# One fused layer: seven small projections moved into TensorE's first wait, scores a turn later, the trace inputs on VectorE alone

## The chip, the cores and the metric

The kernel runs on one core of a Trainium2 chip. The metric is device time in microseconds (us) for one launch; the lower the better. Three runs of the kernel before gave 239.74, 240.85 and 242.25 us, median 240.85.

## The reference, cut to what matters

Eight batches (B = 8) of 128 tokens with 128 channels. The layer has four parts:

```python
# 1 cross attention, 16 heads of 8, masked, plus one "self" score per query
s = softmax([q @ k_prev.T * SCALE masked, (q * k_self).sum(-1) * SCALE])
a = (s[..., :-1] @ v_prev + s[..., -1:] * v_self) @ Wo + bo
# 2 windowed attention (16 tokens back, sigmoid weights), then a layer norm
x1 = x + layernorm(window_attention(a)) * gamma + beta
# 3 conditioning: gate from x1 and its decayed context, modulation from a small network,
#   eight decayed traces over the tokens, each of gate * x1 * modulation_d * blend_d
gated = sigmoid(concat(x1, ctx) @ Wg + bg) * x1          # per token and channel
mod   = sigmoid(gelu(x1 @ Wn1 + bn1) @ Wn2 + bn2) + 0.5    # eight numbers per token
trace = sum_d ema_d(gated * mod[d] * blend[d])   # d = 0..7
z = layernorm((gelu(x1 @ Wsoma) * sigmoid(trace @ Wtemp)) @ Wout)
# 4 a mixture of 8 experts, one per token: out = x1 + gate * ffn_e(z)
```

The change touches parts 1 and 3.

## The kernel before, in words

All engines run hand-written instruction streams that meet at semaphores. There is one list of PSUM jobs, `order`: each small job on TensorE (PE) has a bank and a place in that bank's queue, and waits until the job before it on the bank has been read.

**Front.** Both halves of the batches (four each) are transposed, projected to q and k, split into three bf16 parts by ScalarE (ACT) and VectorE (DVE), and stacked by DMAs from SyncE's queue (SP, L398), 12 for each half. PE may start the first scores only when the stack of half 0 has landed.

**First attention.** A loop over turns `t` does one group of four heads of one batch in each step: `scores_max` (unit t, PE L694), whose row maximum DVE takes (`row_max`, L1436); `scores` (unit t - 8, L717), whose exponential ACT takes (`weights_of`, L1157); `values` (unit t - 10, L731). After the four maxima of a batch DVE computes the negated maximum (`shift`, L1442 to L1444), PE turns it (`turn_shift`, L704, last but the projections in turn 4b + 4), ACT copies it and issues a DMA (L1167) that writes it into the stack; the first `scores` of that batch waits for this DMA (`shift_in`). The list `PREPARE` puts seven jobs of the front into turns 0 to 9: the self scores of both halves (`self_0`, `self_1`, L658), the value projections of both inputs and halves (`vp`, `vs`, L666) and the self k projection of half 1 (`ks_1`, L628). At t = 30 the first half goes over to the window attention (`HANDOFF`), whose stack SP builds anew. The turns go on into the window attention (L829, L832, L843) at `WINDOW_AT`.

**Conditioning.** Of half 0 the transposes, context, gate and hidden jobs lie in the last turns of the window attention. After them PE runs `soma(0)`, `modulation(0)` (L863), `traces(0)` (L907: 8 products of 128x128 in f32, 16 records, per batch), then for half 1 `transpose_x1`, `context`, `hidden`, `soma`, then `traces(1)`, `modulation(1)`, `input_gate(1)` and `traces(2)` to `traces(7)`, with output jobs between them. The inputs of the traces, `Gb`, have four buffers for eight batches. DVE writes six of the eight slices of each (`blended`, L1565, one scalar_tensor_tensor per slice), GpSimd (POOL) the other two in one pair of tensor_tensor (L578, L579; `PD = 2`). `traces(b)` waits for both. On DVE the order is `mod_sums(0)`, `modulate(0)`, `blended(0)`, `add_norm(1)` (the second half of the layer norm: L1511, L1514, L1515), `blended(1)` to `blended(7)`, with the sums of gate and modulation of half 1 after `blended(3)`.

**Rest.** Layer norm, router, a scatter of the rows by expert through memory, and 15 expert tiles.

Of the kernel before, what the change touches and what calls it, by code (L numbers as in the profile page):

```python
# [14 lines left out]
def fused_layer(nc, A, out):  # L15
# [27 lines left out]
    with ctx:  # L43
# [42 lines left out]
        prodT = sb("prodT", [128, HT])  # L86
# [122 lines left out]
        PD = 2  # L209

        GROUPS = (range(0, HALF), range(HALF, NB - 1), range(NB - 1, NB))

        LAG_SCORES, LAG_VALUES = 8, 10
        LAG_PVTR, LAG_OUT = 12, 15
# [3 lines left out]
        PREPARE = {0: "self_0", 1: "vp_0", 2: "vs_0", 3: "ks_1", 7: "self_1", 8: "vp_1", 9: "vs_1"}  # L218
# [11 lines left out]
        def handoff(t, step):  # L230
# [5 lines left out]
                 ("kT_1", 3), ("ks_0", 7)]  # L236
        alternating = []
        for t in range(TURNS):
            if t in PREPARE:
                alternating += [PREPARE[t]]  # L240
# [16 lines left out]
        alternating += ["mod_0", "x1T_1", "ctxT_1", "h1_1", "mod_1", "gate_1",  # L257
# [78 lines left out]
        blend_vector, blend_pool, blend_used, traces_read = sem("blend_vector"), sem("blend_pool"), sem("blend_used"), sem("traces_read")  # L336
# [125 lines left out]
        def _(pool):  # L462
# [106 lines left out]
            job_wait_read(pool, "bl_0")  # L569
            job_wait_read(pool, "bl_1")  # L570
            for b in range(NB):
                k = b % NG
                pool.wait_ge(gated_ready, half_of(b) + 1)
                pool.wait_ge(mod_ready, half_of(b) + 1)
                if b >= NG:
                    pool.wait_ge(blend_used, b - NG + 1)
                ds = slice(ND - PD, ND)
                link(pool.tensor_tensor(Gb[:, k, ds, :], bc_mid(wgate[:, b, :], PD), blend[:, ds, :], ALU.mult))  # L578
                pool.tensor_tensor(Gb[:, k, ds, :], Gb[:, k, ds, :], bc_last(mod[:, b, ds], D), ALU.mult)\  # L579
                    .then_inc(blend_pool, 1)  # L580

# [37 lines left out]
        def _(pe):  # L619
# [32 lines left out]
            def sum_self(half):  # L652
                name = f"self_{half}"
                job_wait_read(pe, f"ks_{half}")
                pe.wait_ge(heads_ready, 1)
                job_wait_free(pe, name)
                for i in range(HALF):
                    m = pe.matmul(bank_of(name)[:, i * H:(i + 1) * H], prodT[:, i * T:(i + 1) * T], heads[:],  # L658
                                  start=True, stop=True)
                job_full(m, name)  # L660
# [45 lines left out]
            def scores(b, g):  # L706
                u = b * G + g
                pe.wait_ge(shift_in[b % 2], 16 * (b // 2 + 1))
                if u == 0:
                    job_wait_read(pe, "qT_1")  # L710
                    job_wait_read(pe, "kT_1")
# [8 lines left out]
            def values(b, g):  # L720
                u = b * G + g
                pe.wait_ge(scores_read, u + 1)
                if u == 0:
                    job_wait_read(pe, "trS2_1")
                    job_wait_read(pe, "trX_1")
# [68 lines left out]
            def prepare(name):  # L794
                what, half = name.split("_")
                half = int(half)
                if what == "ks":
                    project_self_k(half)
                if what == "self":
                    sum_self(half)  # L800
                if what == "vp":
                    job_wait_read(pe, f"trX_{half}")
                    pe.wait_ge(ld_wv, 16)
                    four_batches(name, half, xT, wqkv[:, 2, :])
                if what == "vs":
                    job_wait_read(pe, f"trS2_{half}")
                    four_batches(name, half, s2T, wqkv[:, 2, :])
# [8 lines left out]
            project_self_k(0)  # L816

# [80 lines left out]
            def traces(b):  # L898

                pe.wait_ge(blend_vector, b + 1)  # L900
                pe.wait_ge(blend_pool, b + 1)
# [20 lines left out]
            for t in range(TURNS):  # L922
                if t < UNITS:
                    scores_max(t // G, t % G)
                if t in PREPARE:
                    prepare(PREPARE[t])
# [14 lines left out]
                if t >= NEGM_AT and t % G == 0 and t <= UNITS:  # L941
                    turn_shift(t // G - 1)
# [116 lines left out]
        def _(act):  # L1059
# [159 lines left out]

            act.wait_ge(tau_abs, 1)  # L1220
# [4 lines left out]
            for t in range(TURNS):  # L1225
                for half, name in ((int(n[-1]), n[:2]) for n in (PREPARE.get(t - 1),) if n):
                    if name == "vp":
                        evac_prev_v(half)
                    if name == "vs":
                        evac_self_v(half)  # L1230
# [61 lines left out]
            gelu("soma_1", somaT, 128, BSOMA, 1)  # L1292
            mod_sigmoid(1)
            gate_sigmoid(1)
# [57 lines left out]
        def _(dve):  # L1352
# [50 lines left out]
            def self_product(half):  # L1403

                name = f"ks_{half}"
                job_wait_full(dve, name)
                if half:
                    job_wait_read(dve, "self_0")
                job_read(dve.scalar_tensor_tensor(prodT[:], bank_of(name)[:, 0:HT], cols[:, BK:BK + 1], whole(0, half),
                                                  ALU.add, ALU.mult), name)  # L1410
# [16 lines left out]
            self_product(0)  # L1427

# [129 lines left out]
            def blended(b):  # L1558
# [5 lines left out]
                for d in range(ND - PD):  # L1564
# [11 lines left out]
            for t in range(TURNS + 1):  # L1576
# [8 lines left out]
                if t == G:  # L1585
                    self_product(1)
                if t == 2 * G:
# [148 lines left out]
```

## Time and profile before

| | us |
|---|---|
| runs shown, lowest, median, highest | 239.74, 240.85, 242.25 |
| profiled execution, its own time | 243.61 |
| its span, first to last instruction | 241.9 |
| busy: PE, DVE, ACT, POOL | 179.5, 117.8, 114.9, 74.1 |
| mean granted TensorE clock | 0.852 |

The profiled execution is 2.76 us longer than the median of the three runs shown. Busy shares are averages over the whole span; the rows read for the prediction are from single stretches, in us from the start of the span.

### The profile page before, as it was taken

Reading aid. Unit: us, or ns where it says so; the run is one execution under the profiler, and the core shown is the slowest. Engines: PE = TensorE matmul, PEld = TensorE weight load, DVE = VectorE, ACT = ScalarE, POOL = GpSimd, SP = SyncE. Lnnn points to the kernel's source line nnn. Section 1 sums busy time; section 2 is a strip of 40 time slices with the busy share of each in tenths; the row PEclk is TensorE's granted clock in tenths of the full one; section 3 lists DMA queues with packets and bytes.
Section 4 is the critical chain, followed back from the end, with each engine's and each line's share of the span. In section 5 each row is a group of like instructions: output and inputs, shape, how many; then the busy total and the mean of one; then the engine's idle time right before and its main releaser. Section 6 shows DMA issues by size and latency. Waiting matters only on the chain.

```text
span 241.9 us, 4780 instructions
## 1 busy us (share of the span) xinstructions
PE 179.5 (74%) x1677; PEld 136.0 (56%) x1677; DVE 117.8 (49%) x337; ACT 114.9 (48%) x268; POOL 74.1 (31%) x109
## 2 busy tenths in 40 slices
PE   3771986989979779996999649949951005999990
PEld 2321955767645545653567347948751004999990
DVE  6455391566873631431153598396367101455530
ACT  3664142578757677761555506301374001455550
POOL 8996002000700040000200370070256740155553
PEclk9976595899999799997999959977995555899997
DMA  4455354560000440250000893000000229100000
GB/s 125 112 135 169 101 173 113 155 182 3 7 3 1 144 128 3 84 166 16 3 3 0 297 313 87 0 0 3 0 3 0 87 87 299 42 25 24 24 9 0
DMA packets 21085, 18.91 MB, mean 78 GB/s; under 512 B 4029, under 2 KB 18608, under 8 KB 21062
## 3 DMA queue, kind: packets, MB, share of 16 engines
q1 hardware_dynamic: 19606, 16.86, 23.3%
q0 software_dynamic: 896, 1.59, 1.9%
q8 instruction: 14, 0.23, 0.4%
q10 hardware_dynamic: 560, 0.16, 0.3%
q14 instruction: 9, 0.07, 0.1%
HBM read 8.54 MB, written 4.03 MB: 52 GB/s over the span
## 4 chain that ended last, share of the span: by engine, by line
PE 51%; DMA 15%; SPq 10%; DVE 9%; ACT 4%; issue 4%; POOL 4%; ACTq 0%; DVEq 0%; POOLq 0%
SPq L398 9%; PE ps L1052 6%; PE ps L1039 6%; PE ps L907 5%; DMA t_Ks<-t_parts 5%; PE ps L863 5%; DMA t_Qs<-t_negmT 5%; DVE t_Qs L1565 4%; PE ps L628 4%; PE ps L843 3%; POOL z_dram L606 3%; PE ps L829 3%; PE ps L694 2%; PE ps L731 2%; PE ps L666 2%
## 5 line engine op out<-in xcount | busy, mean ns | idle before, releaser
L1347 ACT ACTIVATE t_v_pad<-ps,t_b_tile 128x128 f32<-128x128 f32 x60 | 17.1, 368 | 33.2 <-PE ps L1039 33.2
L1436 DVE TENSOR_REDUCE t_mx<-ps 128x4 f32<-128x512 f32 x32 | 21.8, 688 | 20.8 <-PE ps L694 20.7
L1189 ACT ACTIVATE t_P<-ps 128x512 f32<-128x512 f32 x32 | 19.1, 603 | 15.3 <-PE ps L832 14.9
L907 PE MATMUL ps<-t_ema,t_Qs 128*128 128x128 f32 x128 | 19.2, 317 | 8.4 <-DVE t_Qs L1565 8.4
L907 PEld LDWEIGHTS ps<-t_ema,t_Qs 128*128 128x128 f32 x128 | 18.6, 230 | 10.5 <-DVE t_Qs L1565 9.4
L1157 ACT ACTIVATE t_P<-ps 128x512 f32<-128x512 f32 x32 | 18.9, 605 | 10.1 <-PE ps L717 5.3
L611 POOL DMA_INDIRECT out_dram<-t_v_pad,t_Qs x15 | 15.1, 1008 | 25.9 <-DVE t_v_pad L1710 25.3
L1565 DVE SCALAR_TENSOR_TENSOR t_Qs<-t_v_pad,t_mod,t_blend 128x128 f32<-128x128 f32 x48 | 19.4, 478 | 0.2
L563 POOL TENSOR_SCALAR t_rstd<-t_mv 128x4 f32<-128x4 f32 (+2 forms) x5 | 1.4, 276 | 55.9 <-DVE t_mv L1505 55.9
L694 PE MATMUL ps<-t_Ks,t_Qs 96*128 96x128 bf16 x128 | 13.9, 237 | 6.0 <-DMA t_Ks<-t_parts 5.3
L1039 PE MATMUL ps<-t_zsT,t_late 128*128 128x128 f32 x120 | 17.7, 296 | 0.2 <-DVE t_zsT L1706 0.2
L1031 PE MATMUL ps<-t_ident,t_Qs 128*128 128x128 f32 x15 | 4.4, 308 | 17.5 <-DMA t_Qs<-z_dram 17.5
L1052 PE MATMUL ps<-t_Ks,t_v_pad 128*128 x120 | 17.0, 286 | 0.0
L1039 PEld LDWEIGHTS ps<-t_zsT,t_late 128*128 128x128 f32 x120 | 16.2, 210 | 0.6 <-DVE t_zsT L1706 0.6
L829 PE MATMUL ps<-t_bandb,t_identb 128*128 128x512 bf16 x32 | 12.8, 400 | 4.2 <-DMA t_Ks<-t_parts 4.2
L694 PEld LDWEIGHTS ps<-t_Ks,t_Qs 96*128 96x128 bf16 x128 | 9.7, 109 | 10.5 <-issue 8.6
L1052 PEld LDWEIGHTS ps<-t_Ks,t_v_pad 128*128 128x128 f32 x120 | 15.0, 196 | 0.3
L717 PE MATMUL ps<-t_Qs,t_Ks 96*128 96x128 bf16 x128 | 13.3, 230 | 2.4 <-DMA t_Qs<-t_negmT 1.4
L843 PE MATMUL ps<-t_P,t_v_pad 128*32 128x128 f32 x256 | 13.7, 290 | 0.0
L731 PE MATMUL ps<-t_P,t_v_pad 128*32 128x128 f32 x256 | 13.6, 289 | 0.0
L832 PEld LDWEIGHTS ps<-t_Qs,t_Ks 96*128 96x128 bf16 x128 | 10.3, 100 | 5.0 <-issue 1.2
L832 PE MATMUL ps<-t_Qs,t_Ks 96*128 96x128 bf16 x128 | 12.9, 225 | 0.0
(266 smaller groups left out, 376.3 us busy)
## 6 DMA issues: line engine op xcount, KB each, us to landing
t_Qs<-t_parts SPq DMA_DIRECT2D x24, 128.0 KB
t_Ks<-t_parts SPq DMA_DIRECT2D x24, 128.0 KB
t_Ks<-in_L_ffn_W_dram SPq DMA_DIRECT2D x1, 2048.0 KB, 9.6
z_dram<-t_empty_row SPq DMA_DIRECT2D x1, 1935.0 KB, 8.3
t_Qs<-z_dram SPq DMA_DIRECT2D x1, 1032.0 KB, 7.9
t_Qs<-z_dram SPq DMA_DIRECT2D x1, 645.0 KB, 5.5
t_rows<-in_fside_BxSxS_dram SPq DMA_DIRECT2D x2, 256.0 KB, 3.1
t_x_tok<-in_x_dram SPq DMA_DIRECT2D x2, 256.0 KB, 3.6
```

Of the source, the lines that this page charges most:

```text
L398: sp.dma_start(stack[2 * slot:KROWS:SPAN, half], parts[:, half, which, part, :])\
L694: m = pe.matmul(MAX_BANKS[u % 2][:, j * T:(j + 1) * T], stacked(Qs, b, h), stacked(Ks, b, h), start=True, stop=True)
L829: pe.matmul(bank[:, :], identb[:], bc_mid(bandb[:], 4), start=True, stop=False)
L832: m = pe.matmul(bank[:, j * T:(j + 1) * T], stacked(Ks, b, h), stacked(Qs, b, h), start=False, stop=(j == 3))
L843: m = pe.matmul(VALUE_BANKS[b % 2][32 * j:32 * j + 32, 0:T], v_pad[:, b, quad_head(g, j), :], P[:, (UNITS + u) % 3, j * T:(j + 1) * T], st ...
L907: m = pe.matmul(ps[group][:, i * T:(i + 1) * T], Gb[:, b % NG, d, :], ema[:, 1 + d, :], start=(d == 0), stop=(d == ND - 1))
L1039: m = pe.matmul(ps[n % 2][:, c * 128:(c + 1) * 128], W1_tile[:, n % 2, c * 128:(c + 1) * 128], zsT[:, n % 2, :], start=True, stop=True)
L1052: m = pe.matmul(o, hsT[:, n % 2, c * 128:(c + 1) * 128], W2[:, bass.ds(e, 1), c, :].rearrange("p a f -> p (a f)"), start=False, stop=(c == ...
L1157: act.activation(P[:, u % 3, :], SCORE_BANKS[u % 2][:, :], ACT.Exp, scale=SCALE).then_inc(scores_read, 1)
L1189: act.activation(P[:, (UNITS + u) % 3, :], ps[u % 4][:, :], ACT.Sigmoid, scale=SCALE).then_inc(window_scores_read, 1)
L1436: dve.tensor_reduce(mx[:, b, 4 * g:4 * g + 4], MAX_BANKS[u % 2][:, :].rearrange("p (j t) -> p j t", j=4), AX.X, ALU.max).then_inc(max_scor ...
L1565: m = dve.scalar_tensor_tensor(Gb[:, b % NG, d, :], wgate[:, b, :], mod[:, b, d:d + 1], blend[:, d, :], ALU.mult, ALU.mult)
```

## The change

- `PREPARE` is gone. PE does its seven jobs right after `project_self_k(0)`, ahead of turn 0, in the order vp_0, ks_1, vs_0, vp_1, vs_1, self_0, self_1. ACT copies the four value projections ahead of its turns, DVE forms both self products ahead of its turns and reads the second self scores at t = 2 in place of t = 8. `prodT` has a buffer for each half. Banks 2 to 7 serve the seven jobs.
- All lags of the first attention grow by one turn: scores 9, values 11, output steps 13 and 16 turns behind the maxima.
- `turn_shift` is ahead of `values` in its turn, where it was behind `values` and the window work.
- DVE writes all eight slices of `Gb`; POOL's loop, its semaphore and PE's wait on it are gone.
- DVE does `add_norm(1)` ahead of `blended(0)`; after `blended(3)` the gate's sum stands ahead of the modulation's; ACT's two sigmoids of half 1 change places too.
- PE does `modulation(0)` ahead of `soma(0)`, then all jobs of half 1 (transposes, context, hidden, gate, modulation, soma), and then the eight traces in a row with the output jobs between them as they were.

```diff
-        LAG_SCORES, LAG_VALUES = 8, 10
-        LAG_PVTR, LAG_OUT = 12, 15
+        LAG_SCORES, LAG_VALUES = 9, 11
+        LAG_PVTR, LAG_OUT = 13, 16
-        PREPARE = {0: "self_0", 1: "vp_0", 2: "vs_0", 3: "ks_1", 7: "self_1", 8: "vp_1", 9: "vs_1"}
...
-                 ("kT_1", 3), ("ks_0", 7)]
+                 ("kT_1", 3), ("ks_0", 7), ("vp_0", 6), ("vs_0", 4), ("ks_1", 3), ("vp_1", 5), ("vs_1", 2),
+                 ("self_0", 6), ("self_1", 7)]
...
-            for b in range(NB):
-                k = b % NG
-                pool.wait_ge(gated_ready, half_of(b) + 1)
-                pool.wait_ge(mod_ready, half_of(b) + 1)
-                if b >= NG:
-                    pool.wait_ge(blend_used, b - NG + 1)
-                ds = slice(ND - PD, ND)
-                link(pool.tensor_tensor(Gb[:, k, ds, :], bc_mid(wgate[:, b, :], PD), blend[:, ds, :], ALU.mult))
-                pool.tensor_tensor(Gb[:, k, ds, :], Gb[:, k, ds, :], bc_last(mod[:, b, ds], D), ALU.mult)\
-                    .then_inc(blend_pool, 1)
...
             project_self_k(0)
+            project_prev_v(0)
+            project_self_k(1)
+            project_self_v(0)
+            project_prev_v(1)
+            project_self_v(1)
+            sum_self(0)
+            sum_self(1)
...
-                pe.wait_ge(blend_pool, b + 1)
...
                 if t < UNITS:
                     scores_max(t // G, t % G)
-                if t in PREPARE:
-                    prepare(PREPARE[t])
...
                     scores(u // G, u % G)
+                if t >= NEGM_AT and t % G == 0 and t <= UNITS:
+                    turn_shift(t // G - 1)
                 u = t - LAG_VALUES
...
-                if t >= NEGM_AT and t % G == 0 and t <= UNITS:
-                    turn_shift(t // G - 1)
...
+            modulation(0)
             soma(0)
-            modulation(0)
-            traces(0)
             transpose_x1(1)
             context(1)
             hidden(1)
+            input_gate(1)
+            modulation(1)
             soma(1)
-            traces(1)
-            modulation(1)
-            input_gate(1)
-            traces(2)
-            for b in range(3, NB):
+            for b in range(NB):
                 traces(b)
...
+            evac_prev_v(0)
+            evac_self_v(0)
+            evac_prev_v(1)
+            evac_self_v(1)
             act.wait_ge(tau_abs, 1)
...
             self_product(0)
+            self_product(1)
...
-                for d in range(ND - PD):
+                for d in range(ND):
                     m = dve.scalar_tensor_tensor(Gb[:, b % NG, d, :], wgate[:, b, :], mod[:, b, d:d + 1],
                                                  blend[:, d, :], ALU.mult, ALU.mult)
...
             mod_sums(0)
             modulate(0)
+            add_norm(1)
             job_wait_read(dve, "bl_0")
             job_wait_read(dve, "bl_1")
-            blended(0)
-            add_norm(1)
-            for b in range(1, NB):
+            for b in range(NB):
                 blended(b)
                 if b == 3:
+                    gate_sums(1)
                     mod_sums(1)
-                    gate_sums(1)
                     modulate(1)
                     gated_inputs(1)
```

## Rows read from the trace of the kernel before

**Rows 1.** The page, part 4: shares of the chain that ended last, by engine.

```profile
PE 51%; DMA 15%; SPq 10%; DVE 9%; ACT 4%; issue 4%; POOL 4%; ACTq 0%; DVEq 0%; POOLq 0%
```

**Rows 2.** Busy time by stretch: start:end, length, engines' busy us, clock, DMA share, GB/s.

```profile
17.84:23.10 5.26, 0.00 (x0) 0.03 (x1) 3.07 (x6) 3.12 (x6) 4.30 (x11) 0.71 0.63 189
23.10:30.90 7.80, 7.80 (x42) 7.26 (x43) 2.85 (x5) 1.86 (x5) 0.00 (x0) 0.54 0.37 100
37.30:43.50 6.20, 4.41 (x27) 3.80 (x28) 0.82 (x2) 2.04 (x7) 1.40 (x4) 0.50 0.35 85
...
137.00:142.37 5.37, 0.04 (x2) 0.00 (x1) 4.87 (x9) 0.23 (x1) 4.73 (x8) 0.73 1.06 358
142.37:146.00 3.63, 3.63 (x17) 3.63 (x18) 3.53 (x8) 0.00 (x0) 1.14 (x2) 0.50 1.06 290
```

**Rows 3.** The chain of waits, two pieces: start, length, what.

```profile
32.12 5.13 DMA t_Qs<-t_negmT
...
47.37 5.96 DMA t_Qs<-t_negmT
```

**Rows 4.** Timeline of PE, first attention: start, length, line, tiles, count, [idle before].

```profile
34.38 1.03 PE L658 MATMUL ps<-t_heads,t_prodT 128*128 128x16 f32 x8 [0.39 <-ACT t_wB L1130]
...
35.83 1.13 PE L666 MATMUL ps<-t_wqkv,t_xT 128*128 128x128 f32 x8 [0.18 <-DVE t_bl_col L1474]
37.30 0.61 PE L717 MATMUL ps<-t_Qs,t_Ks 96*128 96x128 bf16 x4 [0.34 <-DMA t_Qs<-t_negmT]
...
53.38 0.40 PE L717 MATMUL ps<-t_Qs,t_Ks 96*128 96x128 bf16 x4 [1.08 <-DMA t_Qs<-t_negmT]
...
58.95 0.39 PE L717 MATMUL ps<-t_Qs,t_Ks 96*128 96x128 bf16 x4
```

**Rows 5.** Timeline of DVE, conditioning: same columns.

```profile
120.81 1.12 DVE L1511 TENSOR_SCALAR t_rows<-t_rows,t_mv,t_rstd 128x128 f32<-128x128 f32 x4 [1.60 <-POOL t_rstd L564]
...
122.68 0.69 DVE L1515 TENSOR_TENSOR t_rows<-t_rows,t_x_tok 128x512 f32<-128x512 f32 x1
...
137.88 4.44 DVE L1565 SCALAR_TENSOR_TENSOR t_Qs<-t_v_pad,t_mod,t_blend 128x128 f32<-128x128 f32 x6
...
145.67 4.81 DVE L1565 SCALAR_TENSOR_TENSOR t_Qs<-t_v_pad,t_mod,t_blend 128x128 f32<-128x128 f32 x18
...
156.56 8.49 DVE L1565 SCALAR_TENSOR_TENSOR t_Qs<-t_v_pad,t_mod,t_blend 128x128 f32<-128x128 f32 x18
```

**Rows 6.** Timeline of POOL, conditioning: same columns.

```profile
136.47 1.04 POOL L564 TENSOR_TENSOR t_rstd<-t_rstd,t_mhalf 128x4 f32<-128x4 f32 x1
...
142.97 0.61 POOL L579 TENSOR_TENSOR t_Qs<-t_Qs,t_mod 128x256 f32<-128x256 f32 x1
...
161.66 0.61 POOL L579 TENSOR_TENSOR t_Qs<-t_Qs,t_mod 128x256 f32<-128x256 f32 x1
```

**Rows 7.** Timeline of PE, conditioning: same columns.

```profile
145.94 0.79 PE L623 MATMUL ps<-t_ident,t_rows 128*128 128x128 f32 x4
...
149.49 1.95 PE L907 MATMUL ps<-t_ema,t_Qs 128*128 128x128 f32 x16
151.37 1.05 PE L863 MATMUL ps<-t_wn2T,t_Qs 32*128 32x8 f32 x8
...
154.24 3.74 PE L907 MATMUL ps<-t_ema,t_Qs 128*128 128x128 f32 x32
...
171.67 1.95 PE L907 MATMUL ps<-t_ema,t_Qs 128*128 128x128 f32 x16
```

**Rows 8.** Groups of instructions, the row maxima: count, busy us, mean ns, idle before.

```profile
L1436 DVE TENSOR_REDUCE t_mx<-ps 128x4 f32<-128x512 f32 x32 | 21.8, 688 | 20.8 <-PE ps L694 20.7
```

**Rows 9.** The page, part 6: DMA issues, KB each, us to landing.

```profile
z_dram<-t_empty_row SPq DMA_DIRECT2D x1, 1935.0 KB, 8.3
...
t_Qs<-t_negmT ACTq DMA_DIRECT2D x8, 4.0 KB, 1.7
```

**Rows 10.** Timeline of SP's queue: the issue of that large write.

```profile
44.71 0.42 SPq L438 DMA_DIRECT2D z_dram<-t_empty_row  x1
```

More of the change, by code:

```diff
@@ L85, in fused_layer @@
         v_pad = sb("v_pad", [128, NB, H, 32])
-        prodT = sb("prodT", [128, HT])
+        prodT = sb("prodT", [128, 2, HT])
         s_self = sb("s_self", [128, NB, H])
@@ L208, in fused_layer @@
         UNITS = G * NB
-        PD = 2
         GROUPS = (range(0, HALF), range(HALF, NB - 1), range(NB - 1, NB))
-        LAG_SCORES, LAG_VALUES = 8, 10
-        LAG_PVTR, LAG_OUT = 12, 15
+        LAG_SCORES, LAG_VALUES = 9, 11
+        LAG_PVTR, LAG_OUT = 13, 16
         NEGM_AT = G
         EMA_AT = 3 * G
-        PREPARE = {0: "self_0", 1: "vp_0", 2: "vs_0", 3: "ks_1", 7: "self_1", 8: "vp_1", 9: "vs_1"}
         Y0, QK, VW = 1, 2, 5
@@ L235, in fused_layer @@
         order = [("trS2_0", 6), ("trX_0", 7), ("qT_0", 0), ("kT_0", 1), ("trS2_1", 4), ("trX_1", 5), ("qT_1", 2),
-                 ("kT_1", 3), ("ks_0", 7)]
+                 ("kT_1", 3), ("ks_0", 7), ("vp_0", 6), ("vs_0", 4), ("ks_1", 3), ("vp_1", 5), ("vs_1", 2),
+                 ("self_0", 6), ("self_1", 7)]
         alternating = []
         for t in range(TURNS):
-            if t in PREPARE:
-                alternating += [PREPARE[t]]
             if t % G == 2:
@@ L256, in fused_layer @@
                             HIDDEN_AT: ["h1_0"]}.get(t, [])
-        alternating += ["mod_0", "x1T_1", "ctxT_1", "h1_1", "mod_1", "gate_1",
+        alternating += ["mod_0", "x1T_1", "ctxT_1", "h1_1", "gate_1", "mod_1",
                         "tg_0", "o_0", "tg_1", "o_1", "tg_2", "oT_0", "o_2", "oT_1", "lg_0", "lg_1", "rank"]
@@ L335, in fused_layer @@
         mod_sig, mod_ready = sem("mod_sig"), sem("mod_ready")
-        blend_vector, blend_pool, blend_used, traces_read = sem("blend_vector"), sem("blend_pool"), sem("blend_used"), sem("traces_read")
+        blend_vector, blend_used, traces_read = sem("blend_vector"), sem("blend_used"), sem("traces_read")
         gated_soma_ready, z_ready = sem("gated_soma_ready"), sem("z_ready")
@@ L567, in _ @@
             inverse_std(0, range(HALF, NB))
-            job_wait_read(pool, "bl_0")
-            job_wait_read(pool, "bl_1")
-            for b in range(NB):
-                k = b % NG
-                pool.wait_ge(gated_ready, half_of(b) + 1)
-                pool.wait_ge(mod_ready, half_of(b) + 1)
-                if b >= NG:
-                    pool.wait_ge(blend_used, b - NG + 1)
-                ds = slice(ND - PD, ND)
-                link(pool.tensor_tensor(Gb[:, k, ds, :], bc_mid(wgate[:, b, :], PD), blend[:, ds, :], ALU.mult))
-                pool.tensor_tensor(Gb[:, k, ds, :], Gb[:, k, ds, :], bc_last(mod[:, b, ds], D), ALU.mult)\
-                    .then_inc(blend_pool, 1)
             def norm_z(half):
@@ L657, in sum_self @@
                 for i in range(HALF):
-                    m = pe.matmul(bank_of(name)[:, i * H:(i + 1) * H], prodT[:, i * T:(i + 1) * T], heads[:],
+                    m = pe.matmul(bank_of(name)[:, i * H:(i + 1) * H], prodT[:, half, i * T:(i + 1) * T], heads[:],
                                   start=True, stop=True)
@@ L709, in scores @@
                 if u == 0:
-                    job_wait_read(pe, "qT_1")
-                    job_wait_read(pe, "kT_1")
+                    job_wait_read(pe, "vs_1")
+                    job_wait_read(pe, "ks_1")
                 if u >= 2:
@@ L723, in values @@
                 if u == 0:
-                    job_wait_read(pe, "trS2_1")
-                    job_wait_read(pe, "trX_1")
+                    job_wait_read(pe, "vs_0")
+                    job_wait_read(pe, "vp_1")
                 if g == 0:
@@ L792, in weight_job, with project_prev_v, project_self_v @@
                     spread_blend(1)
[L794 to L802, printed above, removed]
+            def project_prev_v(half):
+                job_wait_read(pe, f"trX_{half}")
+                if half == 0:
                     pe.wait_ge(ld_wv, 16)
[L804 to L807, printed above, removed]
+                four_batches(f"vp_{half}", half, xT, wqkv[:, 2, :])
+            def project_self_v(half):
+                job_wait_read(pe, f"trS2_{half}")
+                four_batches(f"vs_{half}", half, s2T, wqkv[:, 2, :])
             transpose_inputs(0)
@@ L924, in _ @@
                     scores_max(t // G, t % G)
-                if t in PREPARE:
-                    prepare(PREPARE[t])
                 if t % G == 2:
@@ L1225, in _ @@
             for t in range(TURNS):
[L1226 to L1230, printed above, removed]
                 if t >= G and t % G == 0 and t <= UNITS:
@@ L1292, in _ @@
             gelu("soma_1", somaT, 128, BSOMA, 1)
+            gate_sigmoid(1)
             mod_sigmoid(1)
-            gate_sigmoid(1)
             def evac_traces(group):
@@ L1406, in self_product @@
                 job_wait_full(dve, name)
-                if half:
-                    job_wait_read(dve, "self_0")
-                job_read(dve.scalar_tensor_tensor(prodT[:], bank_of(name)[:, 0:HT], cols[:, BK:BK + 1], whole(0, half),
+                job_read(dve.scalar_tensor_tensor(prodT[:, half, :], bank_of(name)[:, 0:HT], cols[:, BK:BK + 1], whole(0, half),
                                                   ALU.add, ALU.mult), name)
@@ L1584, in _ @@
                     shift(0)
-                if t == G:
-                    self_product(1)
-                if t == 2 * G:
+                if t == 2:
                     self_scores(1)
```

## The prediction

> **What bounds the kernel now.** I read the chain that ended last first: half of it is PE, but DMA and SP's queue hold a quarter and DVE 9% [rows 1]. So the time is not one engine's sum; it lies in a few stretches where PE waits or runs at half clock, and I read those by stretch. From 17.84 to 23.10 PE does nothing (the stack of half 0 is on its way). From 23.10 to 30.90 it is busy without a gap, but at a granted clock of 0.54; from 37.30 to 43.50 it is at 0.50, the 1.2 GHz level, and busy 4.41 of 6.20 us. From 137.00 to 142.37 it is idle again, and the 3.63 us after that are at 0.50 [rows 2]. The chain of waits says what ended the two waits in the first attention: the DMA that writes a batch's negated maximum, 5.13 us from 32.12 and 5.96 us from 47.37 [rows 3]. In the conditioning it is DVE, which writes the trace inputs [rows 5].
>
> **The change, first attention.** The seven jobs leave the turns and fill PE's first wait. At full clock a value projection costs 1.13 and a self-score job 1.03 us [rows 4]; taking 1.13 for the k projection too, 5 x 1.13 + 2 x 1.03 = 7.7 us. The wait holds 5.26, so the first maxima start at 17.84 + 7.7 = 25.5 in place of 23.10: 2.4 us late. I take full clock since PE would be busy without a gap there. Bounds of this unknown: hidden but for 2.4 us, or twice as long at half clock (15.4, start at 33.2).
> New waits in it: self_1 waits for DVE's second self product, and all maxima are queued behind it on PE; DVE has 2.2 us free there [rows 2]. ACT's four value copies go ahead of its turns and cost nothing: it is idle 2.1 us in the wait and 5.9 of the 7.8 us after it [rows 2]; if that cover were gone, the first exponential would be late.
> Then the maxima run with nothing between them: four by DVE at 0.69 [rows 8], two small copies and the shift, some 3.9 us in all, then 0.7 us to the DMA. It is issued at 30.1, not 32.12. It lands 1.7 us (the median of the eight [rows 9]) to 5.13 us later [rows 3]; I take 5.13, since the stack's second half is still being written. `scores(0)` starts at 35.3, 2.0 us earlier than at 37.30 [rows 4].
> From there the second effect counts. With scores nine behind, `turn_shift(1)` is a turn ahead of this wait on PE instead of behind it, so batch 1's shift is under way meanwhile; self_1 is gone from ahead of the wait, vp_1 and vs_1 from around it. Twelve turns later comes `scores(12)`. Before, four such turns with their weight jobs took 58.95 - 53.38 = 5.57 us [rows 4], 1.39 each; 12 make 16.7, so PE is there at 52.0, and up to 3 us later if the half clock of 37.30 to 43.50 comes back there.
> But batch 3's shift is now issued at about 46, after SP's 1.9 MB write at 44.71 [rows 10], which takes 8.3 us [rows 9], to 53.0. Batch 2's, issued at 47.37, landed at 53.33, right behind it [rows 3]. I let batch 3's land at 53.3 too: `scores(12)` at 53.35 in place of 58.95, **-5.6 us**. Bounds: -7.0 if it does not wait, -2.0 if only the earlier first DMA is left, +0.8 if the seven jobs run at half clock (first DMA at 38, landing by 43, `scores(12)` at 59.7).
> The Trainium skill (DMA: Bandwidth & Descriptors, section Queues, rings and completion order) says that each DMA engine takes turns, packet by packet, between the queues it has work for; by it ACT's small write would pass SP's large one and the gain would be 7.0. The row of batch 2 speaks against it here, so the sum goes by the row.
> The rest of the first attention and the window attention keep their work. All lags, hand-overs and the window's start move by the same one turn, so the extra turn adds no instruction; SP issues the same DMAs in the same order. I let the 5.6 us pass through to the conditioning, and use times of before from here.
>
> **The change, conditioning.** What does a slice cost DVE? Six took 4.44 us beside POOL (0.74 each), 18 took 4.81 us (0.267 each) after POOL had ended at 143.58, and 18 took 8.49 us with POOL until 162.27 (5.7 us at 0.74 and 2.8 at 0.267 make 18) [rows 5, 6]. So DVE is slow only while POOL works on its slices; with POOL's loop gone I take 0.267, so 2.14 us for all eight slices of a batch.
> Modulation ahead of soma makes `mod` ready at about 137.0. `add_norm(1)` waits for POOL's result at 137.51 [rows 6]; behind it on DVE are now all eight batches. It takes 2.56 us (120.81 to 123.37) [rows 5], so x1 of half 1 is there at 140.1 and four batches of slices at 148.7.
> PE goes on at 140.15 with half 1. Those jobs took 3.55 us from 145.94 to 149.49 and 2.87 us from 151.37 to 154.24, 6.4 in all at full clock [rows 7]. After the 5.37 us wait the next 3.63 us were at half clock [rows 2]; the wait is now some 2.9 us and I let it cost the same, 1.8 us. `traces(0)` starts at 148.4, all four buffers full. Two batches of traces take 3.74 us [rows 7]; eight take 15.0, and the three jobs between them about 1.0 each by the 1.03 and 1.13 above: traces(7) ends at 166.4 in place of 171.67 + 1.95 = 173.6: **-7.2 us**.
> DVE stops after the fourth batch, at 148.7, for the sums and sigmoids of half 1, 3.3 us by their order (its sums and product at the 0.69 of a 512-column operation, ACT the rest), and writes the last slice at 161.3; PE wants it at 164, so that is covered by 2.7 us. ACT's wait chain for soma_1 ahead of the sigmoids lies beside PE's traces. Moving two slices from POOL to DVE costs nothing while PE sets the pace. Bounds: PE's half-1 jobs all at half clock (12.8 us) leave -2.4; no half clock and faster DVE make it -9.5.
>
> **Sum.** 243.61 - 5.6 - 7.2 = 230.8 for the profiled execution, which stands 2.76 above the median shown; from the median it is 228.0. I predict 229.4, between them.
>
> **The rivals.**
> 1. The filled wait gives nothing: the seven jobs run at the clock of 23.10 to 30.90, or the first DMA lands no earlier because the stack's second half is in its way. For it: that stretch was busy throughout and still at 0.54 [rows 2]. Against: it began after a wait, and the fill begins after work. The front then gives +0.8 to -2.0: 234 to 237.
> 2. The small write passes the large one, batch 2's 5.96 us having another cause: front -7.0 and full clock in the conditioning. Against it is the coincidence of landings. 224 to 227.
> 3. Slower: DVE's 0.74 is not POOL's doing but the price of these slices beside PE's and ACT's work. Then 64 slices take 47.4 us, DVE ends near 191, traces(7) ends at 192.7, 19 us late; less the front's 5.6 it is 257. It decides from 0.53 us a slice on, where 64 slices eat both gains. Against it are the 18 at 0.267.
> 4. The change saves waits but others take them over, in the two stacks of the window attention or in the chain from o_0 to the router: 239 to 243.
>
> **How the numbers follow.** The forecast, 226 to 234, gets 0.62; rival 1 0.17, rival 2 0.08, rival 4 0.07, rival 3 0.06. The range from 224 to 236.5 takes in both bases and most of rivals 1 and 2, and leaves out 3, 4 and the worst of 1. About 1% is what a measurement of this kernel can tell from no change: below 238.4 lie forecast, 1 and 2, so 0.87 faster; 0.07 the same; 0.06 slower.
>
> **What would show it.** Right: PE busy from 17.84 to about 25.5 at a clock near 1, the first shift's DMA issued near 30, `scores(12)` near 53 and behind the large write; eight L1565 of one batch in 2.1 us with POOL still; traces at 1.87 us a batch in one run, from x1 of half 1 plus 8 us. Wrong: L1565 above 0.5 us, half clock through the fill, `scores(0)` at 37 again, or PE idle between two traces.

## The result, and the profile after

The changed kernel takes **229.45 us** (median of 4 runs, 227.26 to 231.12) against 241.55 us for the kernel before beside it: a ratio of **0.944, 95% interval 0.933 to 0.955**. The forecast was 229.4. The two profiled executions are 243.61 and 228.22 us, 15.4 apart; the forecast for that difference was 12.8. A ratio leaves out the runs that stand far above the fastest of their kernel while a median holds all of them, so the two need not agree (most of all in experiment 8).

I read the stages first: the time at which the same instruction starts in both traces.

| mark | before | after | change |
|---|---|---|---|
| first row maxima | 23.10 | 24.21 | +1.1 |
| scores(0) | 37.30 | 32.78 | -4.5 |
| scores(12) | 58.95 | 51.71 | -7.2 |
| first half handed over (y0T_0) | 73.97 | 65.13 | -8.8 |
| window attention starts | 89.32 | 81.41 | -7.9 |
| x1 of half 0 transposed, conditioning starts | 124.11 | 118.38 | -5.7 |
| traces(7) ends | 173.62 | 159.09 | -14.5 |

So in this pair of traces the first attention gains 8.8 us, of which 5.7 arrive at the conditioning, and the conditioning gains 8.8 (49.51 us from its start to the end of traces(7) before, 40.71 after). The last 0.9 us come behind it. It is one trace of each kernel, and the same code spreads by 1 to 4 us a stage from trace to trace; the end of the section on experiments shows it.

The chain of the changed kernel: DMA's share is 8% where it was 15%, PE's 59% where it was 51% [rows 1].

```profile
PE 59%; DVE 12%; DMA 8%; SPq 7%; issue 5%; POOL 4%; ACT 4%; DVEq 0%; POOLq 0%
```

PE's timeline after (start, length, line, tiles, count, [idle before]):

```profile
18.07 1.05 PE L649 MATMUL ps<-t_wqkv,t_xT 128*128 128x128 f32 x8
...
22.50 1.86 PE L641 MATMUL ps<-t_heads,t_prodT 128*128 128x16 f32 x16
24.21 0.61 PE L677 MATMUL ps<-t_Ks,t_Qs 96*128 96x128 bf16 x8
...
32.78 0.63 PE L700 MATMUL ps<-t_Qs,t_Ks 96*128 96x128 bf16 x4
...
51.71 0.39 PE L700 MATMUL ps<-t_Qs,t_Ks 96*128 96x128 bf16 x4
...
81.41 0.38 PE L814 MATMUL ps<-t_bandb,t_identb 128*128 128x512 bf16 x1 [2.40 <-DMA t_Ks<-t_parts]
...
104.33 0.61 PE L814 MATMUL ps<-t_bandb,t_identb 128*128 128x512 bf16 x1 [2.53 <-DMA t_Ks<-t_parts]
...
134.46 1.12 PE L606 MATMUL ps<-t_ident,t_rows 128*128 128x128 f32 x4 [2.71 <-DVE t_rows L1492]
...
142.23 9.09 PE L891 MATMUL ps<-t_ema,t_Qs 128*128 128x128 f32 x80
...
152.02 3.73 PE L891 MATMUL ps<-t_ema,t_Qs 128*128 128x128 f32 x32
...
157.14 1.95 PE L891 MATMUL ps<-t_ema,t_Qs 128*128 128x128 f32 x16
```

The wait from 17.84 on is full of work and the maxima follow at 24.21; scores(0) at 32.78 and scores(12) at 51.71 have no wait recorded, where in [rows 4] the DMA of the maxima ended a wait at scores(0) and again at 53.38, at scores(8). From 142.23 the traces run without a gap.

Busy time by stretch, after (start:end, length, PE, PEld, DVE, ACT, POOL busy, clock, DMA share, GB/s):

```profile
18.00:24.20 6.20, 6.20 (x51) 5.64 (x50) 3.73 (x7) 4.30 (x10) 3.81 (x11) 1.00 0.55 167
28.30:33.00 4.70, 3.88 (x29) 2.85 (x29) 3.82 (x11) 1.43 (x7) 0.00 (x0) 0.50 0.53 173
33.00:43.00 10.00, 10.00 (x90) 8.08 (x88) 5.56 (x14) 5.10 (x15) 1.44 (x4) 0.55 0.44 124
...
81.41:86.90 5.49, 5.49 (x53) 3.06 (x54) 0.86 (x4) 2.83 (x6) 0.57 (x1) 0.69 0.01 3
104.30:110.30 6.00, 5.97 (x44) 3.20 (x45) 0.77 (x3) 1.95 (x4) 0.00 (x0) 0.51 0.01 3
134.40:138.30 3.90, 3.84 (x14) 2.71 (x14) 3.87 (x15) 1.55 (x3) 0.00 (x0) 0.60 1.05 297
142.20:159.00 16.80, 16.80 (x141) 15.91 (x139) 12.95 (x49) 5.64 (x9) 0.00 (x0) 1.00 0.00 1
```

The fill ran at 1.00, but the half clock (0.50, the 1.2 GHz level) did not go: it moved to 28.3 to 42, and it stands behind both waits of the window attention and behind the wait for x1. Before, the stretches that answer to the two window rows, the second first, were better off:

```profile
112.00:118.00 6.00, 6.00 (x63) 3.54 (x60) 0.77 (x3) 2.87 (x6) 0.00 (x0) 0.72 0.01 3
89.32:95.00 5.68, 5.68 (x68) 3.42 (x69) 0.87 (x4) 4.22 (x9) 1.58 (x1) 1.00 0.01 3
```

DVE's timeline after, conditioning:

```profile
131.83 1.12 DVE L1488 TENSOR_SCALAR t_rows<-t_rows,t_mv,t_rstd 128x128 f32<-128x128 f32 x4 [0.43 <-POOL t_rstd L560]
...
134.44 8.49 DVE L1542 SCALAR_TENSOR_TENSOR t_Qs<-t_v_pad,t_mod,t_blend 128x128 f32<-128x128 f32 x32
...
146.03 6.39 DVE L1542 SCALAR_TENSOR_TENSOR t_Qs<-t_v_pad,t_mod,t_blend 128x128 f32<-128x128 f32 x24
```

32 slices in 8.49 us are 0.265 each, and so are the 24: the 0.74 of [rows 5] is gone.

### The profile page after: what moved, and what is told of

It is laid out like the page before. It is cut to its first block, busy times and chain, and to the rows that moved or that the text cites. A ratio compares the mean times of both kernels' runs of the same rounds, so it can differ in the third digit from the quotient of the medians.

```text
span 226.5 us, 4763 instructions
## 1 busy us (share of the span) xinstructions
PE 176.7 (78%) x1677; PEld 132.3 (58%) x1677; DVE 115.2 (51%) x353; ACT 115.0 (51%) x268; POOL 63.3 (28%) x93
## 3 DMA queue, kind: packets, MB, share of 16 engines
q1 hardware_dynamic: 19606, 16.86, 24.9%
## 4 chain that ended last, share of the span: by engine, by line
PE 59%; DVE 12%; DMA 8%; SPq 7%; issue 5%; POOL 4%; ACT 4%; DVEq 0%; POOLq 0%
PE ps L1018 7%; SPq L394 6%; PE ps L1031 6%; PE ps L891 6%; PE ps L611 5%; PE ps L848 5%; DMA t_Ks<-t_parts 4%; PE ps L828 4%; PE ps L677 4%; PE ps L814 3%; PE ps L606 3%; POOL z_dram L589 3%; DVE t_mx L1413 3%; PE ps L817 3%; PE ps L714 2%
## 5 line engine op out<-in xcount | busy, mean ns | idle before, releaser
L814 PE MATMUL ps<-t_bandb,t_identb 128*128 128x512 bf16 x32 | 13.5, 421 | 4.9 <-DMA t_Ks<-t_parts 4.9
L1542 DVE SCALAR_TENSOR_TENSOR t_Qs<-t_v_pad,t_mod,t_blend 128x128 f32<-128x128 f32 x64 | 17.1, 347 | 0.1
L891 PEld LDWEIGHTS ps<-t_ema,t_Qs 128*128 128x128 f32 x128 | 14.8, 192 | 1.2 <-issue 1.0
L677 PE MATMUL ps<-t_Ks,t_Qs 96*128 96x128 bf16 x128 | 14.4, 248 | 1.3 <-DVE t_mx L1413 1.3
L891 PE MATMUL ps<-t_ema,t_Qs 128*128 128x128 f32 x128 | 14.8, 275 | 0.0
L828 PE MATMUL ps<-t_P,t_v_pad 128*32 128x128 f32 x256 | 14.6, 306 | 0.0
L714 PE MATMUL ps<-t_P,t_v_pad 128*32 128x128 f32 x256 | 14.4, 301 | 0.0
L817 PEld LDWEIGHTS ps<-t_Qs,t_Ks 96*128 96x128 bf16 x128 | 10.9, 106 | 5.5 <-issue 2.2
L700 PE MATMUL ps<-t_Qs,t_Ks 96*128 96x128 bf16 x128 | 14.0, 239 | 0.0
L817 PE MATMUL ps<-t_Qs,t_Ks 96*128 96x128 bf16 x128 | 13.8, 236 | 0.0
```

Of the source, the lines that this page charges most:

```text
L677: m = pe.matmul(MAX_BANKS[u % 2][:, j * T:(j + 1) * T], stacked(Qs, b, h), stacked(Ks, b, h), start=True, stop=True)
L714: m = pe.matmul(VALUE_BANKS[b % 2][32 * j:32 * j + 32, g // 2 * T:(g // 2 + 1) * T], v_pad[:, b, pair_head(g, j), :], P[:, u % 3, j * T:(j ...
L814: pe.matmul(bank[:, :], identb[:], bc_mid(bandb[:], 4), start=True, stop=False)
L817: m = pe.matmul(bank[:, j * T:(j + 1) * T], stacked(Ks, b, h), stacked(Qs, b, h), start=False, stop=(j == 3))
L828: m = pe.matmul(VALUE_BANKS[b % 2][32 * j:32 * j + 32, 0:T], v_pad[:, b, quad_head(g, j), :], P[:, (UNITS + u) % 3, j * T:(j + 1) * T], st ...
L891: m = pe.matmul(ps[group][:, i * T:(i + 1) * T], Gb[:, b % NG, d, :], ema[:, 1 + d, :], start=(d == 0), stop=(d == ND - 1))
```

## Experiments

**1 and 2: each half of the change alone.** The first has the first attention of the changed kernel with the conditioning of the one before; the second the reverse.

```
1:  after; PE, ACT and DVE orders of the conditioning and POOL's two slices as before
2:  before; those orders as after, POOL's loop gone, DVE writes all ND slices
```

> The front of the changed kernel (seven jobs in the first wait, lags 9/11/13/16, turn_shift ahead of values) with the conditioning of the kernel before. Theory: the two parts add up; the front delivers what stands at the first transposes of x1, 124.11 - 118.38 = 5.7 us, so about 235.8 us against 241.5 of before and 229.5 of the change. Rival: the front's 8.8 us at the first hand-over (73.97 against 65.13) arrive whole, 232.7 us; or what is saved in front is waited for in the conditioning, 241 us.

> The conditioning of the changed kernel (all slices on DVE, add_norm(1) first, PE's half-1 jobs ahead of the traces) with the front of the kernel before. Theory: -8.8 us (traces(7) starts 14.53 us earlier in the change, of which 5.73 come from ahead of the conditioning): about 232.7 us. Rival: the conditioning gains less on its own because its clock depends on what comes before it, 235 to 237 us.

Measured: the front alone 235.33 (233.61 to 238.09), ratio 0.980 [0.970, 0.990]; the conditioning alone 237.93 (236.22 to 239.60), ratio 0.987 [0.977, 0.997]. The first came as expected, the second 5 us above it and nearer to the rival's 235 to 237. Its trace says in part why: from the conditioning's start to the end of traces(7) it took 41.88 us, 7.6 less than before, but it began at 126.14, 2.0 us later than in the trace of before with the same code ahead of it. The two ratios give 4.9 and 3.2 us, less than the 13.6 of the whole; each is uncertain by 2.4, so I do not read a cause into the missing part. One thing does show: with the conditioning code of before, the first took 46.40 us for that stage, not 49.51. What the marks show is safer: each half does its part where it was put (hand-over at 67.75 in the first, 7.6 us off the stage in the second).

**3 and 4: what in the conditioning.** The third gives POOL its two slices of a batch back and keeps all new orders; the fourth keeps DVE alone and takes the old orders.

```
3:  after, and   for d in range(ND - PD): ...   # DVE, PD = 2
                 pool.tensor_tensor(Gb[:, k, ds, :], ...) x2 a batch
4:  after, and   PE, DVE, ACT orders of before
```

> The change with POOL writing two of the eight slices of each batch as before, all orders as in the change. Theory (POOL's work slows DVE's slices to 0.74 us): six slices of batch 4 take 4.4 us again, PE waits some 2.5 us ahead of traces(4): 231.5 to 232.5 us. Rival (0.74 has another cause): DVE has two slices less per batch, 1.6 us, and the time is that of the change, 229.5, or a little below.

> The change with DVE alone writing all slices, but DVE's, ACT's and PE's orders of the conditioning as before (blended(0) ahead of add_norm(1), traces(0) and traces(1) among the half-1 jobs). Theory (POOL's share was most of the conditioning's price): 0.5 to 1 us above the change, 230 to 230.5 us. Rival (the order brings most of the 8.8 us): 234 to 236 us.

Measured: 232.30, ratio 0.962 [0.955, 0.969], as expected; and 227.74, ratio 0.939 [0.928, 0.950], some 2.3 us below the expectation and far from its rival. The stage took 44.81 (in the third's longest run, 236.05) and 43.36 us, against 40.71 with both and 49.51 with neither. So in the trace POOL's slices cost 4.1 us under the new order, and the new order gives 2.7 under DVE alone (2.8 and 1.3 against the slowest trace of the changed conditioning, 42.04 us). In the runs only the first shows: the fourth's interval holds the changed kernel's 0.944, and its trace reached the conditioning 3.1 us earlier (115.25) with the same code ahead of it, which covers the 2.7. What the order is worth in time stays open.

The third also shows a loss that I had not put down to POOL. Its slices now start while DVE is still at the layer norm (DVE, groups by line, 125 to 165 us: count, busy, mean ns, idle before):

```profile
L1503 DVE TENSOR_SCALAR t_rows<-t_rows,t_mv,t_rstd 128x128 f32<-128x128 f32 x4 | 2.8, 761 | 0.4 <-POOL t_rstd L561 0.4
```

Four of these take 1.12 us in [rows 5] and in the changed kernel, 2.8 here. POOL slows the norm too, and x1 with it: PE waits 5.11 us for x1 of half 1, where the changed kernel has 2.71, and only 1.00 ahead of traces(4), where 2.5 was expected.

**5 and 6: scores nine behind, and the place of the shift.**

```
5:  LAG_SCORES, LAG_VALUES = 8, 10;  LAG_PVTR, LAG_OUT = 12, 15   # after: 9, 11, 13, 16
6:  turn_shift(...) behind window_values(...) again               # after: behind scores(...)
```

> The change with the old lags (scores 8, values 10, output 12 and 15 turns behind), all else as in the change; turn_shift stays ahead of values but comes behind scores in its turn. Theory: at lag 8 the shift of batch 1 waits again behind scores(0) on PE, and PE waits again for the DMAs of batches 1 and 2: scores(0) as in the change (32.8), the first hand-over 2 to 3 us later than the change's 65.1, the time 231 to 232.5. Rival (DVE's maxima set the pace of the first attention): hand-over at 65, time as the change, 229.5.

> The change with turn_shift behind values and the window work in its turn, as before, lags 9. Theory: the DMA of a batch is issued one values job (0.36 us) later and has a turn to spare, so nothing moves: hand-over at 65 to 66, time 229 to 230. Rival (the shift's place is what took the waits away): PE waits for a shift's DMA again and the hand-over comes 2 us later, 231.5.

Measured: 230.25, ratio 0.950 [0.940, 0.959]; and 228.72, ratio 0.937 [0.928, 0.946]. Neither can be told from 0.944. The hand-over came 1.4 us later with the old lags (66.57), a little less than expected, and 2.8 later with the shift moved back (67.89, where nothing was expected to move), and both were gone by the start of the conditioning (116.99 and 118.05, where the changed kernel has 118.38). Traces of one and the same front hand over up to 2.7 us apart, so neither difference is clear of that. The waits tell more. With the old lags PE waits for a shift's DMA again, at scores(12); with the shift moved back it waits 0.23 us for one there, and 1.32 us for the conditioning's weights ahead of it:

```profile
52.27 0.40 PE L700 MATMUL ps<-t_Qs,t_Ks 96*128 96x128 bf16 x4 [1.12 <-DMA t_Qs<-t_negmT]
```

```profile
42.03 1.11 PE L606 MATMUL ps<-t_ident,t_wc_raw 128*128 128x128 f32 x4 [1.32 <-DMA t_b_raw<-in_L_ffn_b_dram]
...
54.86 0.40 PE L700 MATMUL ps<-t_Qs,t_Ks 96*128 96x128 bf16 x4 [0.23 <-DMA t_Qs<-t_negmT]
```

So in these traces the extra turn takes a wait of PE away; that it, or the shift's place, brings time is not shown.

**7: unneeded work in the late waits of PE.** Matmuls whose results are overwritten go ahead of the two waits for the window attention's stacks (10 each) and ahead of x1 of half 1 (11). But for the place of two semaphore waits, they change nothing but what PE does while it waits.

```
+ def keep_busy(bank, n):
+     for _ in range(n):
+         pe.matmul(bank[:, :], identb[:], bc_mid(identb[:], 4), start=True, stop=True)
  ...
+ keep_busy(bank, 10)
  pe.wait_ge(stack_in[half_of(b)], 16 * (4 * NSLOT + 2))
```

> The change with unneeded matmuls (128 x 512, bf16, into a free bank, 10, 10 and 11 of them, about 2.2 us at full clock) in PE's three late waits: for the two window stacks and for x1 of half 1. They add work and take none away. Theory (what the front gained was lost again to stretches at 1.2 GHz behind these waits): from the window's start to the first transposes of x1 the stretch shrinks from 37.0 us to 34.5 or less, the half-1 jobs after x1 take 6.4 in place of 7.8 us, time 225 to 226.5. Rival (clock falls anyway, or the extra matmuls delay the work behind them): 229.5 to 231.5.

Measured: **224.61** (222.51 to 232.16), ratio 0.924 [0.916, 0.931]. The stretches that answer to the window rows and the x1 row above:

```profile
80.34:86.00 5.66, 5.66 (x68) 3.43 (x69) 0.86 (x4) 3.88 (x8) 0.00 (x0) 1.00 0.01 3
102.00:108.00 6.00, 5.87 (x76) 3.63 (x76) 0.84 (x4) 3.14 (x6) 0.00 (x0) 1.00 0.01 3
129.70:136.10 6.40, 6.37 (x40) 4.81 (x41) 6.39 (x25) 3.70 (x5) 0.00 (x0) 1.00 1.05 293
```

All three are at 1.00. In the second, 76 matmuls of the kernel's own fit into the 6.0 us that held 44. The way from the window's start to the conditioning takes 33.3 us instead of 37.0, and half 1's jobs 6.4 instead of 7.8. Of the 3.1 us that the front's gain lost on its way, 0.9 lie ahead of the window's start and 2.2 behind it, and there the filled waits give 3.7 back: in this pair of traces it was half clock behind these waits.

**8 and 12: the same in the early waits.** The eighth adds two such matmuls in each of turns 1 to 8. The twelfth adds to that eight ahead of the wait for the conditioning's weights, and SP issues their loads three places earlier.

```
8:   after scores_max in turns 1 to 8:  keep_busy(ps[3], 2)
12:  8, and  keep_busy(bank_of("wC1"), 8);  pe.wait_ge(ld_wcr, 16 * 7)
     and SP: wc_raw, wn1_raw, wn2_raw, b1_raw ahead of b_raw, gamma1, beta1
```

> As the run with unneeded matmuls in the three late waits, and two more in each of turns 1 to 8, where PE waits for DVE's maxima. Theory: the stretch from 28.3 to 43 us, at half clock in the change, runs at full clock; twelve turns from scores(0) take 15.5 in place of 18.9 us; hand-over near 62.5, time 222.5 to 224. Rival: PE there waits for ACT, DVE or the large write's end (51.9 us) instead, hand-over at 64 to 65, and the time is that of the run with three filled waits.

> As the run with unneeded matmuls in all waits; the seven loads of the conditioning's weights go three places ahead in SP's queue, and eight unneeded matmuls fill what is left of PE's wait for them in turn 14. Theory (that wait of 3.7 us let the clock fall to half for 33 us): granted clock 1.00 from 24 us to the hand-over, hand-over at 58 to 60, time 216 to 219. Rival (the clock falls in the first attention without a wait, too): hand-over at 64 to 78 from run to run and a spread of 10 us as before.

The eighth missed: 231.69 (222.15 to 236.86), ratio 0.935 [0.926, 0.944], no better than the changed kernel. Its profiled execution, one of the long ones with 236.45 us, shows one place where the time went. The clock was full until PE waited 3.70 us for a load of weights:

```profile
41.16 1.12 PE L606 MATMUL ps<-t_ident,t_wc_raw 128*128 128x128 f32 x4 [3.70 <-DMA t_b_raw<-in_L_ffn_b_dram]
```

and for the 33 us behind that wait it was at half clock, though busy 32.84 of them (stretches of the same kernel):

```profile
24.00:37.00 13.00, 11.64 (x131) 7.14 (x128) 11.00 (x31) 5.69 (x19) 0.00 (x0) 1.00 0.43 130
37.00:41.00 4.00, 0.40 (x4) 0.23 (x4) 1.21 (x3) 1.66 (x4) 1.40 (x4) 0.93 0.46 128
41.00:74.00 33.00, 32.84 (x287) 23.22 (x287) 15.69 (x47) 16.33 (x44) 4.36 (x16) 0.50 0.24 69
74.00:76.00 2.00, 2.00 (x34) 1.25 (x32) 1.70 (x5) 1.19 (x2) 0.00 (x0) 0.87 0.00 0
```

The shortest of its eight runs, 222.15 us, is near the time expected; this is what one long one shows. The changed kernel, at half clock from 28.3 to 42, comes to the same transposes at 41.01 and finds the loads landed. The twelfth fills half of that last wait (1.92 us are left): **221.18** (220.82 to 223.53), ratio **0.919 [0.912, 0.926]**, the lowest time found, and its six runs lie within 2.8 us of each other. The interval overlaps that of experiment 7, so what the early fills add to the late ones is not shown, but for the narrow spread.

```profile
24.00:41.50 17.50, 14.16 (x147) 8.46 (x146) 12.20 (x32) 7.75 (x23) 0.00 (x0) 1.00 0.43 120
41.50:65.20 23.70, 22.69 (x343) 16.09 (x344) 17.84 (x56) 17.53 (x51) 5.80 (x20) 1.00 0.37 101
65.20:130.50 65.30, 61.41 (x671) 36.07 (x669) 24.29 (x76) 39.85 (x77) 5.45 (x9) 1.00 0.26 84
130.50:153.70 23.20, 23.18 (x180) 20.73 (x180) 20.73 (x78) 9.34 (x14) 0.00 (x0) 1.00 0.31 87
```

The clock is 1.00 from 24 to 154. But the expectation missed by 2 us in time, and in the part on the loads: the hand-over came at 65.21, not at 58 to 60. The weights still ended PE's wait only at 41.50, since SP issued the last of their loads at 39.42, later than the 37.50 of the changed kernel in spite of its earlier place; what made SP's queue later is open. At full clock PE waits there for SP's queue. So no cost of the half clock of 28.3 to 42 shows at the hand-over of the changed kernel (65.13 there): PE comes to the weights at 41.01 with it and at 41.50 without.

**9: the fill alone taken back.** The seven jobs return to turns 0 to 9; lags, shift and conditioning stay as after.

```
PREPARE = {0: "self_0", 1: "vp_0", 2: "vs_0", 3: "ks_1", 7: "self_1", 8: "vp_1", 9: "vs_1"}
LAG_SCORES, LAG_VALUES = 9, 11;  LAG_PVTR, LAG_OUT = 13, 16
```

> The change without the filled wait: the seven jobs stay in turns 0 to 9 as before, all else (lags 9, turn_shift ahead of values, conditioning) as in the change. Theory: the first maxima start at 23.1 at half clock with the jobs between them, scores(0) near 36 in place of 32.8, hand-over near 69 in place of 65 to 68, time 232 to 234. Rival (the lag and the shift's place bring the front's gain alone): hand-over at 66 to 67, time as the change, 228 to 230.

Measured: 234.00 (231.84 to 235.56), ratio 0.967 [0.954, 0.979], in time as expected: some 5.6 us slower than the changed kernel by the ratios. scores(0) came at 41.54, 5.5 us behind the expectation, and the hand-over 2.5 behind it:

```profile
71.49 1.10 PE L614 MATMUL ps<-t_attnT,t_wo 128*128 128x512 f32 x2
```

The hand-over comes at 71.49, not at 65.13. Of the 8.8 us gained there, 6.4 are the fill's by these traces, and 2.5 what the lag and the earlier shift give without it. Against the latest hand-over of the same front, 67.75, the fill still gives 3.7; the 2.5 are within the spread.

**10: does a small write wait behind a large one?** In the kernel before, SP's 1.9 MB write goes behind the window stacks in SP's queue.

```
- sp.dma_start(z_dram..., bc_mid(empty_row[:], TILES)).then_inc(z_zeroed, 16)   # its place before
+ (the same line, just ahead of)  sp.wait_ge(b_out, 16)
```

> The kernel before with the 1.9 MB write to memory moved behind the stacks of the window attention in SP's queue. Theory (a small write from ACT's queue lands behind the large one): batch 2's shift lands 1.7 to 2.5 us after its issue in place of 5.96, PE does not wait for it, and that scores unit starts about 1.1 us earlier. Rival (the two queues are served in turns and the 5.96 us have another cause): 5 to 6 us again.

One run, 243.31 us. The tile of the shifts in it and, for comparison, in the kernel before; then PE at scores(8), which in [rows 4] starts at 53.38 after 1.08 idle:

```profile
DMA to landing us min/median/max: 1.7/1.7/3.7
```

```profile
DMA to landing us min/median/max: 1.7/1.7/6.0
```

```profile
51.67 0.39 PE L717 MATMUL ps<-t_Qs,t_Ks 96*128 96x128 bf16 x4
```

The longest landing, now that of the first shift, falls from 6.0 to 3.7 us; batch 2's own falls from 5.96 to 1.8, and the wait is gone: scores(8) starts 1.7 us earlier, of which 0.46 lay ahead of it already. It was the large write that held batch 2's shift. The total did not move: the conditioning started at 127.71, later than the 124.11 of before, with other stretches at half clock.

**11: which work of POOL slows DVE?** Into the changed kernel, 12 unneeded products on POOL (two operands read) beside the slices of batches 0 to 3, and 24 memsets (nothing read) beside those of 4 to 7.

```
+ for i in range(12): pool.tensor_tensor(w_raw[:, 0:2, :], w_raw[:, 0:2, :], w_raw[:, 1:3, :], ALU.mult)
  ...
+ for i in range(24): pool.memset(w_raw[:, 0:2, :], 0.0)
```

> The change with unneeded work on POOL: twelve tensor_tensor of 128 x 256 that read two operands, beside the slices of batches 0 to 3, and twenty-four memsets of the same size, beside those of batches 4 to 7. Nothing waits for them but POOL's later work. Theory (POOL's reading slows VectorE's two-operand slices): 0.7 us a slice beside the tensor_tensor, 0.27 beside the memsets. Rival 1 (any POOL work does it): 0.5 us or more beside both. Rival 2 (POOL is not the cause): 0.27 beside both.

One run, 237.39 us. DVE and then POOL in the same kernel:

```profile
137.16 14.91 DVE L1551 SCALAR_TENSOR_TENSOR t_Qs<-t_v_pad,t_mod,t_blend 128x128 f32<-128x128 f32 x32
...
154.29 6.39 DVE L1551 SCALAR_TENSOR_TENSOR t_Qs<-t_v_pad,t_mod,t_blend 128x128 f32<-128x128 f32 x24
```

```profile
137.30 9.63 POOL L569 TENSOR_TENSOR t_w_raw<-t_w_raw 128x256 f32<-128x256 f32 x12 [2.77 <-DVE t_rows L1501]
154.38 8.79 POOL L572 MEMSET t_w_raw<- 128x256 f32 x24 [7.45 <-DVE t_v_pad L1537]
```

Beside the memsets a slice costs 6.39 / 24 = 0.266 us, as with POOL idle. Of the first 32, those in the 5.1 us after POOL's end make some 19 at 0.266; so some 13 fell into POOL's 9.63 us, about 0.75 each. What counts is that POOL reads, not that it works. The Trainium skill (SBUF — State Buffer, section Who interferes with whom) has this as a rule: a DVE instruction with two inputs in SBUF contends with a GpSimd instruction that reads SBUF, not with one that only writes it. The trace agrees, with 0.75 us against 0.266.

**The same code from trace to trace.** Many of these kernels share a stage word for word, so their traces show how far one stage spreads by itself (us; numbers are those of the experiments):

| stage | kernels with the same code there | time |
|---|---|---|
| to the hand-over, front of before | before; 2 | 73.97; 75.38 |
| to the hand-over, front of after | after; 1, 3, 4, 11 | 65.13; 67.75, 67.27, 65.09, 66.39 |
| window's start to conditioning | before; 2 | 34.8; 34.8 |
| the same | after; 1, 3, 4, 5, 6, 9, 11 | 37.0; 34.4, 36.3, 34.8, 34.6, 34.5, 36.3, 38.3 |
| the same, its waits filled | 7, 8, 12 | 33.3, 33.4, 33.1 |
| conditioning of before | before; 1, 10 | 49.5; 46.4, 46.4 |
| conditioning of after | after; 2, 5, 6, 9 | 40.7; 41.9, 42.0, 41.7, 40.7 |
| the same, its wait filled | 7, 8, 12 | 39.3, 39.3, 39.3 |

The front gains 6 to 10 us at the hand-over and the conditioning 4.3 to 8.8, whichever pair is taken. The loss in the window attention is not a steady one: it took no longer than before in four of the eight kernels of its second row. With the waits filled the same stretches are the shortest, and within 0.3 us of each other.

## Why the prediction was right, and where its sizes were off

**The fill** was to cost 7.7 us at full clock and delay the maxima by 2.4. At full clock it ran, but it took 6.1 us, from 18.07 to 24.21, and the delay was 1.1: two sums of self scores cost 1.86 together, not 2.06, and the five projections some 0.9 each in a row, where the 1.13 of [rows 4] had a start and an end of its own. Experiment 9 shows that the fill carries most of the front.

**The first shift** was issued at 28.75, not 30.1, and had landed by 32.78, within 4.0 us where I took 5.13. So scores(0) came 2.5 us before the forecast.

**scores(12)** was to be held by the large write until 53.35; it came at 51.71. The mechanism was there, only earlier: SP issued that write 1.33 us earlier (43.38), it landed at 51.9, and batch 3's shift, issued at 45.66 beside it, landed 5.9 us later, at 51.6. PE came just then and shows no wait. Experiment 10 shows that the large write holds such a small one. The Trainium skill (DMA: Bandwidth & Descriptors, section Queues, rings and completion order) has each DMA engine take turns between the queues; that the small write would pass, as the prediction drew from it, is not borne out for these two queues. What holds it is not shown: in experiment 7 such a write, issued at 45.14, landed after 5.4 us, some 2.3 ahead of the large one. Rival 2 had the right size for the front by another cause.

**"I let the 5.6 us pass through"** is the step that did not hold in this pair of traces. At the hand-over the gain was 8.8; at the conditioning it was 5.7. So the front's 5.7 met the forecast's 5.6 by two errors that cancel, some 3 us more won and some 3 lost, and that is luck. The first wait for a window stack grew (2.40 us, where before had 1.39), the second did not (2.53, before 2.80), and the clock behind them fell to 0.69 and 0.51, from 1.00 and 0.72. Experiment 7 gives back 3.7 us in just that stretch. That is a small rival 4 inside the forecast case, though not in every trace: in experiments 1, 4, 5 and 6 the stretch took no longer than before. And the half clock of 28.3 to 42 was not in the sum, only in a bound (up to 3 us late at scores(12)): I feared it inside the fill, and it came after it, when PE stood in the turns for DVE's maxima and shift.

**The conditioning** was to give 7.2 us and gave 8.8 in this pair of traces, but only 4.3 to 5.7 against the 46.4 of experiments 1 and 10, which ran this code of before at a clock of 0.93 where the trace of before had 0.86; so the size of this term is not settled. In times of before (5.73 added to those of after), x1 of half 1 was ready at 140.17, forecast 140.1; the traces began at 147.96, forecast 148.4, with 7.8 us of half 1's jobs against 8.2; and they ended at 164.8, forecast 166.4. The traces are the term that was mis-sized: 16.86 us from first to last with the three jobs between, where I had 18.0. That 0.74 is POOL's doing and not DVE's own price, which rival 3 disputed, is shown by the changed kernel itself (0.265 with POOL still) and by experiments 3 and 11. That POOL also slowed the layer norm when it ran beside it was not in the prediction. One bound was mis-added: half-1 jobs of 12.8 in place of 8.2 us leave -2.6 of the -7.2, not -2.4.

**The sum** was 2.6 us short for the profiled execution. The number predicted lay between two bases; against the medians of the runs side by side (241.55 and 229.45, 12.1 apart) the forecast of 12.8 was 0.7 too large, so that 229.4 met 229.45 is in part luck.

## What to carry to other kernels

Follow a gain to the next wait: in the traces read here, 3 of 8.8 us won early were lost on the way, most of them behind later waits, where PE went on at half clock. Before you read a few microseconds of one stage as the effect of a change, see how far the same code spreads there. A wait of PE that can't be removed is worth filling, with work of the kernel, and failing that with unneeded matmuls: filling three late waits took the ratio from 0.944 to 0.924, and filling early ones too to 0.919, which can't be told from 0.924. And before two engines share elementwise work, read what one instruction costs beside the other engine and alone: POOL's two slices of a batch saved DVE 0.5 us and cost it 0.47 on each of the other six.

## What the runs showed of the hardware

- PE can stay at half clock through long unbroken work: 33 us at 0.50 while busy 32.84 (experiment 8), behind a wait of 3.70 us. With half of that wait filled the clock stayed at 1.00 from 24 to 154 us (experiment 12).
- A 4 KB write of ACT's queue landed 5.96 us after its issue with a 1.9 MB write of SP's under way, and the same one after 1.8 us without it (experiment 10). It is not the only thing that holds such a write: the first one took 5.13 us in the kernel before, ahead of the large write.
- DVE's slices cost about 0.75 us beside reads of POOL and 0.266 beside its memsets; four layer-norm products 2.8 us beside POOL, 1.12 alone.
